# A kernel of cross-attention and eight routed experts: other blocks of lanes for the last two experts, a sum handed to GpSimd, and a copy made in halves

## What is computed

```python
x = x + xattn(layernorm(x), ctx, Wq, bq, Wk, bk, Wv, bv)      # (8,128,128), ctx (8,120,128)
n = layernorm(x)
top_vals, top_idx = top_k(n @ gate_w.T, 2); top_w = softmax(top_vals)
h = silu(einsum('td,ehd->eth', n, w1)) * einsum('td,ehd->eth', n, w3)   # 8 experts, hidden 512
y = sum over the token's two experts of top_w * (h @ w2[e].T)
out = x + y
```

## Time and profile before

| | |
|---|---|
| median of 3 runs | 117.87 us |
| lowest, highest | 117.69, 119.39 us |
| the profiled execution | 117.93 us |
| its span, first to last instruction | 116.2 us |
| busy: TensorE, VectorE, ScalarE, GpSimd | 78%, 61%, 45%, 40% of the span |

### The profile page before, as it was taken

One profiled execution on the slowest core, in us unless ns is written; L12 is line 12 of the kernel. 1 busy time (PEld: TensorE's weight loads), 2 busy tenths in 40 slices (PEclk: granted clock), 3 DMA queues, 4 the chain that ended last, 5 costly groups with the idle time before them and its releaser, 6 DMA issues.

```text
span 116.2 us, 1829 instructions
## 1 busy us (share of the span) xinstructions
PE 90.3 (78%) x548; PEld 74.4 (64%) x548; DVE 70.4 (61%) x235; ACT 52.6 (45%) x140; POOL 46.8 (40%) x68
## 2 busy tenths in 40 slices
PE   6997999979799300029999989734999999999960
PEld 2553897736598200029988969322978989899950
DVE  6894668989479100026945758321752998854892
ACT  3116398999782000015927993502541737363000
POOL 7159230832777777600000057770360348720000
PEclk9999999999999955555999999995579999999999
DMA  2969999999411111238200001110310000108233
GB/s 45 342 252 432 426 415 290 292 367 415 166 48 49 66 46 46 69 103 238 81 0 0 0 23 34 48 37 23 91 51 0 23 6 28 54 22 258 103 90 90
DMA packets 7401, 15.01 MB, mean 129 GB/s; under 512 B 1072, under 2 KB 5680, under 8 KB 6496
## 3 DMA queue, kind: packets, MB, share of 16 engines
q1 hardware_dynamic: 5440, 12.17, 30.3%
q0 software_dynamic: 1120, 2.03, 5.6%
q10 hardware_dynamic: 832, 0.71, 2.0%
HBM read 10.09 MB, written 4.80 MB: 128 GB/s over the span
## 4 chain that ended last, share of the span: by engine, by line
PE 41%; another core or an unknown queue 19%; DVE 15%; issue 7%; ACT 6%; DMA 5%; POOL 3%; ACTq 0%; DVEq 0%; POOLq 0%
PE bank L1199 8%; PE bank L1160 6%; PE bank L1163 5%; PE bank L1161 5%; DMA w_sb<-parts 3%; PE bank L1018 3%; DVE x L991 2%; PE bank L1101 2%; PE bank L1146 2%; DMA parts<-qT,xg 2%; PE bank L1210 2%; POOL parts L432 2%; PE bank L1055 2%; DVE x L709 2%
## 5 line engine op out<-in xcount | busy, mean ns | idle before, releaser
L1160 PE MATMUL bank<-xgT,w_lo 128*128 128x288 f32 x64 | 24.4, 382 | 14.2 <-ACT xgT L559 12.8
L1160 PEld LDWEIGHTS bank<-xgT,w_lo 128*128 128x128 f32 x64 | 13.2, 207 | 16.7 <-ACT xgT L559 13.7
L432 POOL DMA_INDIRECT parts<-qT,xg x12 | 12.1, 1007 | 24.6 <-ACT qT L579 19.9
L1163 PE MATMUL bank<-xgT,w_hi 128*128 128x288 f32 x64 | 20.2, 315 | 0.0
L1161 PE MATMUL bank<-xgT,w_hi 128*128 128x288 f32 x64 | 20.0, 313 | 0.0
L565 ACT ACTIVATE xn<-bank 128x288 f32<-128x288 f32 x32 | 13.1, 408 | 14.9 <-remote 7.7
L410 POOL DMA_INDIRECT expert_rows<-tok,slot x16 | 15.7, 979 | 8.7 <-issue 4.6
L884 DVE TENSOR_TENSOR kT<-bank,xn 128x288 f32<-128x288 f32 x24 | 10.8, 451 | 9.8 <-ACT xn L565 6.6
L876 DVE TENSOR_TENSOR xgT<-bank,xgT 128x288 fp32r<-128x288 f32 x8 | 3.6, 456 | 17.5 <-ACT xgT L559 15.8
L1161 PEld LDWEIGHTS bank<-xgT,w_hi 128*128 128x128 f32 x64 | 13.3, 207 | 0.7
L1163 PEld LDWEIGHTS bank<-xgT,w_hi 128*128 128x128 f32 x64 | 13.1, 205 | 0.6 <-DVE xgT L876 0.4
(11 more groups left out here) (183 smaller groups left out, 179.0 us busy)
## 6 DMA issues: line engine op xcount, KB each, us to landing
w_sb<-in_w1T SPq DMA_DIRECT2D x2, 1024.0 KB, 10.0
w_sb<-in_w3T SPq DMA_DIRECT2D x2, 1024.0 KB, 11.9
w_sb<-in_w2T SPq DMA_DIRECT2D x2, 1024.0 KB, 20.0
expert_rows<-xg SPq DMA_DIRECT2D x1, 1179.0 KB, 19.3
xg<-expert_rows SPq DMA_DIRECT2D x8, 147.4 KB, 3.9
parts<-w_hi SPq DMA_DIRECT2D x1, 1024.0 KB
w_sb<-parts SPq DMA_DIRECT2D x2, 512.0 KB, 4.3
x_sb<-in_x SPq DMA_DIRECT2D x2, 256.0 KB, 4.4
```

Source lines behind the costliest of these rows:

```text
L432: nc.gpsimd.indirect_dma_start(parts[:, :], bass.IndirectOffsetOnAxis(ap=xg[:, e, k, D:D + 1].bitcast(U32), axis=0), y_sb[e % NY][0:L, k * ...
L1160: mm(ps[:, 0:CAP], w_lo[k][:, at], xT[:, 0, :], start=True, stop=False)
L1163: return mm(ps[:, 0:CAP], w_hi[k][:, at], xT[:, 1, :], start=False, stop=True)
```

## The change

Three edits, and what follows from them.

1. **Lanes.** The 288 tokens of experts 6 and 7 lie in blocks of 128, 128 and 32 lanes instead of three of 96. The blocks of 32 of both experts share one tile of 64 lanes (`home_rest`, `y_rest`). Their rows are loaded to a new tile `xl` with two DMAs per expert. `put_prev` brings only its two blocks of 128 home; the shared block goes with `put_last`, which now also waits for `s_prevlo` and `s_prevhome` in full. The down products of the last expert give 128, 128 and 64 rows.
2. **Sums.** GpSimd, after its scatters, makes the two additions of the second half (`part` of group 1, then `x1`); VectorE keeps those of the first half, and waits for `s_pre[1]` before quarter 2.
3. **Copy.** `turn_xn(0)` becomes two calls of two tiles, into two PSUM banks, and ScalarE copies them as two pieces of 256 columns; `scores(0)` starts on the first piece.

```diff
-            for e in (KP, *range(KP), *range(KP + 1, E)):
+            for e in (KP, *range(KP), *range(KP + 1, PREV)):
                 sp.dma_start(xg[:, e, :, :], region_rows(e)).then_inc(s_xg[e], 16)
+            for e in (PREV, LAST):
+                at = AHEAD + e * REG
+                sp.dma_start(xl[:, e - PREV, 0:2, :],
+                             expert_rows[at:at + 2 * P, :].rearrange("(k p) r -> p k r", k=2)).then_inc(s_xg[e], 16)
+                sp.dma_start(xl[lanes_of(e, 2), e - PREV, 2, :],
+                             expert_rows[at + 2 * P:at + CAP, :]).then_inc(s_xg[e], 16)
...
+            p = grp(part, 1)
+            pool.wait_ge(s_part[1], 16)
+            nc.gpsimd.tensor_tensor(p[:, :, 0, :], p[:, :, 0, :], p[:, :, 1, :], ALU.add).then_inc(s_half[1], 1)
+            pool.wait_ge(s_half[1], 1)
+            nc.gpsimd.tensor_tensor(grp(x1, 1), grp(x1, 1), p[:, :, 0, :], ALU.add).then_inc(s_pre[1], 1)
...
-            def copy_xnT(g):
-                act.wait_ge(s_turn, g + 1)
-                nc.scalar.activation(grp(xnT, g), ps_xn[g][:, :], ACT.Copy).then_inc(s_xnT, 1)
+            def copy_xnT():
+
+                for h in range(2):
+                    act.wait_ge(s_turn, h + 1)
+                    nc.scalar.activation(quarter(xnT, h), ps_xn[h][:, 0:2 * P], ACT.Copy).then_inc(s_xnT, 1)
...
             last_low()
-            for g in range(G):
-                parts_of(g)
-                put_together(2 * g)
-                put_together(2 * g + 1)
+            parts_of_first()
+            for q in range(B // 2):
+                put_together(q)
...
+                    if g == 0 and t % 2 == 0:
+                        pe.wait_ge(s_xnT, t // 2 + 1)
                     last = mm(ps_s[g][:, k * C:(k + 1) * C], xnT[:, t, :], kT[:, t, :], start=True, stop=True)
...
-                    for k in range(KT):
-                        mm(ps_home[q][:, at:at + 2 * D], home_prev[k][:, t * P:(t + 1) * P], y_prev[:, k, :, :],
+                    for k in range(2):
+                        mm(ps_home[q][:, at:at + 2 * D], home[0][k][:, t * P:(t + 1) * P], y_home[0][k],
                            start=(t % 2 == 0 and k == 0), stop=False)
...
                 if q == 0:
-                    pe.wait_ge(s_home, KT)
+                    pe.wait_ge(s_home, 3)
+                    pe.wait_ge(s_prevlo, 3)
+                    pe.wait_ge(s_prevhome, 3)
```

More of the change, by code:

```diff
@@ L530, in _ @@
             copy_kT(1)
-            copy_xnT(0)
+            copy_xnT()
             softmax(0)
@@ L1026, in values, with turn_xn @@
                 last.then_inc(s_v, 1)
-            def turn_xn(g):
+            def turn_xn(lo, hi, ps):
                 pe.wait_ge(s_zero, 5)
-                for t in range(g * TG, (g + 1) * TG):
-                    k = t % TG
+                for t in range(lo, hi):
+                    k = t - lo
                     pe.wait_ge(s_xn, t + 1)
-                    last = nc.tensor.transpose(ps_xn[g][:, k * P:(k + 1) * P], xn[:, t, :], ident[:, :])
+                    last = nc.tensor.transpose(ps[:, k * P:(k + 1) * P], xn[:, t, :], ident[:, :])
                 last.then_inc(s_turn, 1)
@@ L1111, in _ @@
             keys(1)
-            turn_xn(0)
+            for h in range(2):
+                turn_xn(2 * h, 2 * h + 2, ps_xn[h])
             scores(0)
-            turn_xn(1)
+            turn_xn(TG, B, ps_xn[2])
             values(0)
@@ L1150, in turn_rows @@
             def turn_rows(e):
-                pe.wait_ge(s_xg[e], 16)
+                pe.wait_ge(s_xg[e], 16 if e < PREV else 32)
                 pe.wait_ge(s_xgT, e)
+                if e >= PREV:
+                    for k in range(3):
+                        b = lanes_of(e, k)
+                        last = nc.tensor.transpose(ps_xT[:, k * P:min((k + 1) * P, CAP)], xl_of(e, k, 0, D), ident[b, b])
+                    last.then_inc(s_xT, 1)
+                    return
                 for k in range(KT):
@@ L1189, in down @@
                 if e == LAST:
-                    for k in range(KT):
-                        last = mm(ps_last[k][0:L, 0:D], hT[c][:, k * L:(k + 1) * L], w2_sb[:, at], start=(c == 0),
-                                  stop=(c == HC - 1))
+                    for k in range(3):
+                        lanes = slice(k * P, (k + 1) * P) if k < 2 else slice(CAP - 2 * REST, CAP)
+                        last = mm(ps_last[k][0:lanes.stop - lanes.start, 0:D], hT[c][:, lanes], w2_sb[:, at],
+                                  start=(c == 0), stop=(c == HC - 1))
                         if c == HC - 1:
@@ L1208, in turn_out @@
                     pe.wait_ge(s_ysb, KT * e)
+                w = L if e < PREV else P
                 for k in range(KT):
-                    last = nc.tensor.transpose(ps_yr[0:L, k * D:(k + 1) * D], yT[e % 2][:, k * L:(k + 1) * L],
+                    lanes = slice(k * w, min((k + 1) * w, CAP))
+                    last = nc.tensor.transpose(ps_yr[0:lanes.stop - lanes.start, k * D:(k + 1) * D], yT[e % 2][:, lanes],
                                                ident[:, :])
```

98 lines of the change are left out of this document (57 added, 41 removed).

## The result

The changed kernel takes 122.16 us (median of 4 runs, 121.28 to 122.45), the kernel before 118.41 us in the same comparison (4 runs, 117.69 to 119.39): ratio 1.0299, 95% interval 1.0196 to 1.0401. It is slower by 3.75 us, where 117.2 us with a range of 116.3 to 118.3 was forecast.

What follows compares the result with a forecast made beforehand. VectorE was taken to bound the end. The copy's 0.2 us and the sums' 0.55, less 0.1 for GpSimd's hindrance, with the lanes at 0, gave 117.87 - 0.65 = 117.2 us, range 116.3 to 118.3.

Steps and rivals of the forecast that it cites:

- the price of edit 1: Lanes at TensorE's end: eight matmuls fewer, 0.96 us, worth nothing while VectorE is later; price 0.
- the new ends of the quarters: TensorE bringing the last experts home: quarters end at about 108.2, 108.7, 110.4 and 111.3 us instead of 112.29.
- The signs of being wrong: In the changed profile: GpSimd rows well above 1.4 us, no VectorE gap, or loads or last scatter not moving as expected.
- rival A: At the end, GpSimd's additions are too slow and VectorE waits for them: 119.7 us if each takes double; chance 0.12.
- Edit 2, the sums: At VectorE's end, GpSimd takes two additions of 1.27 us each, and quarter 2 starts 0.55 us earlier.
- the gap that GpSimd ends: VectorE idle between quarters 1 and 2, from 110.74 to 111.7 us, about 0.9 us, until GpSimd's sums are done.
- a side effect appeared that I had bounded by 0.1 us: VectorE's additions with two SBUF inputs could hold up GpSimd's start at the end, costing 0.1 us of the gain.
- rival B: At the end, GpSimd is done by 110.7 us and VectorE stays the bound: 116.2 us; chance 0.1.
- Edit 3, the halves: At the front, ScalarE's copy in two pieces lets the scores start 0.21 us earlier; gain taken as 0.2 us.
- C (the middle moves on its own): TensorE's pauses between 38 and 51 us shift independently: 117.4 us, or up to 118.7; chance 0.18 for over 0.4 us.

Runs made afterwards that it cites:

- e6_k64: The kernel before, with only the third matmul of each three in `put_last` reading 64 of its 96 lanes: 101.11 us against 97.99, ratio 1.0315.
- e4_full: The changed kernel with every matmul of the last two experts on 128 rows and columns, zeros between: 98.94 us against 99.3, ratio 0.9952.
- e7_lanes_full: The kernel before with the lanes alone, every matmul of the last two experts on 128 rows and columns: 99.56 us against 97.99, ratio 1.0048.
- e8_grouped: The changed kernel with `put_last` making each quarter's four matmuls of 128 rows first, then both of 64: 99.23 us against 97.99, ratio 1.0118.
- e10_overlap: e2_sums with VectorE also waiting for the second half of `part`, so that its sums run beside GpSimd's: one run, 99.89 us.
- e2_sums: The kernel before with the second half's two additions on GpSimd, nothing else changed: 97.83 us against 99.3, ratio 0.9985.
- e9_quarters: The kernel before with the copy in halves and GpSimd's sums cut by quarters, without the lanes: 98.84 us against 98.45.
- e12_full_quarters: e4_full with GpSimd's sums cut by quarters, against the kernel before: 98.42 us against 98.33, ratio 0.9872.
- e11_before: The kernel before, unchanged, run on one of the other chips for its trace: one run, 99.42 us.
- e5_changed_again: The changed kernel, unedited, on another chip against the kernel before: 101.27 us against 97.99.

## Why the prediction was wrong, step by step

**The step that failed** is the price of edit 1: "the columns that stream stay at 128, so I price them equal", and its sum, "Price 0". `put_last` wasn't priced at all: the new ends of the quarters go on giving each of its matmuls 0.12 us. The working looked at how many matmuls there are and how many columns stream, and never at the blocks' rows and columns beside their neighbours'. What the runs show in its place, on the first chip, is 3.95 us more for TensorE:

- `put_last` makes eight changes to 64 rows and back: 1.43 us in the first half (2.87 against 1.44) and 1.34 in the second (114.43 to 117.37 against 110.69 to 112.29).
- The last expert's down products, whose third block has 64 columns, take 1.37 us more: four groups with one change and back in each, 0.34 us.
- Turning expert 6's rows in, with its block of 32 lanes, takes about 0.3 us more (0.48 us until the next matmul against 0.20). Another 0.37 us arise between there and the turn back of that expert, where the rows of expert 7 are turned in the same way (0.49 us until the next matmul).
- One small block paid nothing: expert 6 is turned back with a third block of 32 columns, and the next matmul follows after 0.24 us (103.61 to 103.85), before after 0.25 us (101.83 to 102.08). Why it paid nothing stays open.
- The 0.96 us saved are real and much smaller: 0.84 us in the changed kernel's two groups of `put_prev`.

Three things say it is the change of shape: in e6_k64 one matmul of three with fewer rows is enough, in e4_full and e7_lanes_full the loss goes when the shapes are made full, and in e8_grouped half the changes cost about half.

The Trainium skill (TensorEngine Tiling (Array Packing), Tiling Modes, Key Properties) states that a change of tiling mode, as opposed to a change of tile, drains TensorE. The traces agree in that each change to 64 rows costs time, about 0.35 us there and back; that it is spent draining they don't show. The page gives no price. The prediction did not weigh it, though it speaks against this very edit. Blocks of 96 paid nothing beside full ones in any trace here: three home matmuls take 0.36 us with 96 rows and 0.35 to 0.36 us with 128 (e4_full, from its second three on), and the last down products 1.88 us with 96 columns (104.41 to 106.29) and 1.92 us with 128 (e7_lanes_full).

**The second error was that of the margin.** The prediction said that TensorE was "only 0.7 us or so ahead" of VectorE's quarter 3, and then gave no rival in which TensorE becomes the bound. All rivals that ended slower were GpSimd's or the middle's. By its own figures the changed kernel had 1.3 us of cover at quarter 2 (home at 110.4 us, needed at 111.7). That is a quarter of the 5.0 us it gave the home stream (106.29 to 111.3 us), and this stream took 7.93. The edge deserved a chance of its own. The signs of being wrong had the same hole: GpSimd's 1.61 us is over the 1.4 us that was to speak for rival A, although GpSimd was not what ended the wait, and no sign stood for TensorE.

**Edit 2, the sums: right, where it can be seen.** In e4_full GpSimd's additions took 1.29 and 1.28 us beside VectorE's PSUM additions (1.27 taken), and the gap that GpSimd ends was 0.91 us (0.96 forecast, 110.74 to 111.7), so the gain at VectorE's end was 0.53 us (6.28 - 5.75) for 0.55. In the changed kernel the mechanism never came to bear, as VectorE was waiting for TensorE. There a side effect appeared that I had bounded by 0.1 us: TensorE's delay made the last expert's rows and so VectorE's sums late, these then overlapped GpSimd's, and each of the two engines slowed the other (VectorE 0.69 to 1.65 us, GpSimd 1.29 to 1.37 and 1.61). It cost nothing at the end, because VectorE waited for TensorE another 1.39 us behind it. In e10_overlap, where it is in the open, VectorE's end grew from 5.75 to 6.84 us. The Trainium skill (GPSIMD Engine Reference, Key points) names this contention for instructions of VectorE with two SBUF inputs; the traces agree, and the factor they show for VectorE is 2.4 to 2.6.

**What edit 1 would have been good for.** I said that TensorE's 0.96 us would matter only if GpSimd were done early (rival B), because of quarter 3. In e2_sums and e9_quarters it is quarter 2 that TensorE brings late, 0.91 and 1.00 us behind VectorE, so that faster sums are worth nothing without fewer matmuls in `put_prev`. With them and full shapes, quarters of the sums shorten VectorE's end by another 0.40 us (e12_full_quarters against e4_full), where they did nothing in e9_quarters.

**Edit 3, the halves: by the front a run gets, near the forecast or three times as much, and invisible at the end.** I took 0.21 us from a front in which ScalarE was busy with the keys until 10.85 us. In fronts of that kind the scores start at 11.37 us with halves (e8_grouped) and at 11.48 without (e7_lanes_full), 0.11 us, and the first scatter at 28.16 and 28.31 us, 0.15 us for 0.2. In the other kind ScalarE waits for the transposes, and halves brought the scores forward by 0.61 us. The two kinds part at the four matmuls for the keys: they take 3.41 us from 6.85 us in the kernel before and 1.88 us from 6.40 us in e11_before. The granted clock reads 1.00 in both from 0 to 12 us, so what makes the difference stays open. It is not the kernel: e11_before is the same kernel (scores at 9.97 us), and the changed kernel had this kind too (scores at 9.35 us, first scatter at 26.67 us against 28.31). So most of the 1.64 us by which its scatters began earlier is not the edit's, and in the middle of expert 3, at 75 us, 0.23 us of them were left.

**The rivals.** A (GpSimd too slow) did not happen: 1.28 to 1.62 us for 128x512 in all traces, never 2.54. B (VectorE stays the bound) did not happen either. C (the middle moves on its own) did, on the first chip: the first pause ended 1.5 us earlier (ScalarE's copy at 49.66 instead of 51.13 us), the second was longer (TensorE idle 4.85 us from 75.4 us, where before it was idle for 2.03 and 1.71 us), and behind it TensorE was 1.12 us late. That is part of the 3.0% measured there. I take it for no part of the change, since no trace from another chip has such pauses; that the change doesn't touch them on the first chip is not shown. On another chip edit 1 alone costs 3.8% (1.0377), and on a third the changed kernel's lowest run is 2.6 us above that of before.

## What to carry to other kernels

Before splitting a matrix stream into blocks of other sizes, list rows and columns of every matmul in order, and count the places where a small block stands beside a full one; each change to 64 rows or columns and back cost here as much as three whole matmuls of 256 columns (0.35 against 3 x 0.12 us). Pad the small block to full size with zeros if that costs nothing else, or else group the small ones together. And when an edit to the second-latest engine is priced at nothing, write down how many microseconds of cover that rests on, and give the case that it runs out a chance.

## What the hardware showed that I had not expected

- A change between a full block and one of 64 rows and back cost TensorE about 0.35 us at a granted clock of 1.00 (106 to 118 us of the changed kernel): the first small one starts 0.33 us after the pair ahead of it and not 0.24, and the next full one follows it after 0.31 us and not 0.12 (110.50, 110.83, 111.14 us; before 107.81, 108.05, 108.17). The pair behind a small one takes 0.43 us until the next small one (111.14 to 111.57). Blocks of 96 rows didn't pay it.
- Two-input additions from SBUF on VectorE and GpSimd at once: 1.65 to 1.81 us for 0.69, and up to 1.62 us for 1.29. The order decides who pays. Where VectorE's addition had begun, it kept 0.69 us and GpSimd's grew (1.37 us in the changed kernel, begun 0.23 us before VectorE's end; 1.53 us in e5_changed_again, begun 0.41 us before it). Where GpSimd's had begun, VectorE's ended 0.55 or 0.56 us behind GpSimd's, in the changed kernel, e5_changed_again, e8_grouped and twice in e10_overlap. VectorE's additions with one input in PSUM kept their time (1.66 us for four) beside GpSimd.
- Where it ran mattered more than any edit here. The kernel before took 118.41 us on the first chip and between 97.99 and 99.3 us in the median on four others. On the first, TensorE worked 0.82 us between 38 and 51 us, at a granted clock of 0.62; in e11_before 11.53 us, at 1.00. The two long pauses that rival C turned on are absent there. What causes them on the first chip stays open: the chain of waits there names only another core or an unknown queue, and none of the experiments met such pauses again.
